# One of a step's fourth powers moves from ScalarE to VectorE, in the last of four attention loops

## The reference, cut to what matters

```
a = jnp.einsum('bhnd,bhmd->bhnm', q, k) ** degree      # degree 4
a = jnp.tril(a)
denom = jnp.sum(a, axis=-1, keepdims=True)
return jnp.einsum('bhnm,bhmd->bhnd', a / denom, v)
```

## Time and profile before

| what | value |
|---|---|
| median of 3 runs | 1062.55 us (1060.91 to 1063.41) |
| the profiled execution's own time | 1058.89 us |
| its span | 1057.1 us |
| busy in the span | PE 940.5 us (89%), DVE 716.9 (68%), ACT 570.6 (54%), POOL 529.0 (50%) |
| fourth powers, ScalarE (line 985) | 160 instructions, 74.8 us, 481 ns mean |
| fourth powers, VectorE (line 1568) | 96 instructions, 56.1 us, 609 ns mean |
| the fourth loop | from 428.3 to 517.7 us of the span |

### The profile page before, as it was taken

How to read it: one execution, slowest core, us unless ns; L and a number is a source line. 1 busy time by engine, 2 the same in 40 slices (tenths; PEclk the granted TensorE clock), 3 DMA queues, 4 the chain that set the end, 5 groups by cost and what they waited for, 6 DMA issues and landing times.

```text
span 1057.1 us, 21153 instructions
## 1 busy us (share of the span) xinstructions
PE 940.5 (89%) x5788; PEld 454.0 (43%) x5789; DVE 716.9 (68%) x1614; ACT 570.6 (54%) x1044; POOL 529.0 (50%) x749
## 2 busy tenths in 40 slices
PE   7989999899898999887788889999999999989992
PEld 5443334334343434342244445455455444444450
DVE  3887976787889778748848666555656565555561
ACT  2358884788847886777445234434344443333340
POOL 0006664564526665557402304665676665656642
PEclk9998999999999999967889899999999999999996
DMA  8213333434323443745458896998999898878884
GB/s 307 86 40 120 121 120 120 171 129 160 122 101 130 150 154 129 301 157 188 154 170 266 311 322 203 224 219 205 224 227 225 222 217 207 199 199 201 210 205 70
DMA packets 76301, 192.53 MB, mean 182 GB/s; under 512 B 10000, under 2 KB 11152, under 8 KB 74960
## 3 DMA queue, kind: packets, MB, share of 16 engines
q1 hardware_dynamic: 58544, 149.05, 42.0%
q0 software_dynamic: 17696, 42.72, 20.3%
HBM read 130.91 MB, written 60.83 MB: 181 GB/s over the span
## 4 chain that ended last, share of the span: by engine, by line
PE 31%; issue 14%; DVE 14%; DMA 13%; ACT 11%; POOL 8%; POOLq 5%; DVEq 3%; SPq 0%; ACTq 0%
DMA out<-yy,sidx 11%; PE bank L518 8%; PE bank L812 5%; PE bank L594 4%; PE bank L583 4%; ACT arena L993 3%; POOL wr L1202 3%; POOLq L1245 2%; PE bank L833 2%; POOLq L1201 2%; PE bank L533 1%; ACT s_p L985 1%; POOL s_p L1167 1%; DMA x1r<-x_scratch 1%; DVE s_p L1568 1%
## 5 line engine op out<-in xcount | busy, mean ns | idle before, releaser
L812 PE MATMUL bank<-arena,xgT 128*128 (+1 forms) x1140 | 283.4, 386 | 4.3 <-ACT xgT L1129 3.1
L1167 POOL TENSOR_TENSOR s_p<-s_p,c_causal 128x128 f32<-128x128 f32 x256 | 148.6, 604 | 218.3 <-DVE s_p L1568 187.2
L1122 ACT ACTIVATE hT<-bank 128x512 f16<-128x512 f16 x95 | 56.7, 597 | 280.6 <-PE bank L822 280.6
L518 PE MATMUL bank<-arena 128*128 128x512 f32 x384 | 184.6, 630 | 11.6 <-ACT arena L947 4.6
L812 PEld LDWEIGHTS bank<-arena,xgT 128*128 128x128 f16 x1140 | 107.4, 99 | 127.9 <-issue 39.7
L1175 POOL TENSOR_TENSOR arena<-arena 128x768 f16<-128x768 f32 x68 | 116.4, 1712 | 90.5 <-ACT arena L890 90.1
L1226 POOL DMA_INDIRECT out<-yy,sidx x79 | 126.7, 1604 | 36.5 <-issue 30.1
L833 PE MATMUL bank<-wd,hT 128*128 128x512 f16 x570 | 140.5, 383 | 0.7 <-ACT hT L1122 0.7
L993 ACT ACTIVATE arena<-bank 128x512 f32<-128x512 f32 (+3 forms) x256 | 101.2, 440 | 59.6 <-PE bank L568 59.6
L1881 DVE TENSOR_SCALAR yy<-bank,hsc 128x512 f32<-128x512 f32 x79 | 59.3, 751 | 107.7 <-DMA out<-yy,sidx 107.5
L518 PEld LDWEIGHTS bank<-arena 128*128 128x128 f32 x384 | 73.4, 199 | 103.2 <-issue 89.2
(11 more groups left out here) (196 smaller groups left out, 1389.1 us busy)
## 6 DMA issues: line engine op xcount, KB each, us to landing
wd<-w_scratch SPq DMA_DIRECT2D x81, 512.0 KB
arena<-w_experts SPq DMA_DIRECT2D x34, 768.0 KB, 5.9
w_scratch<-arena SPq DMA_DIRECT2D x34, 768.0 KB, 4.5
arena<-w_scratch SPq DMA_DIRECT2D x17, 1024.0 KB, 8.2
xin<-x SPq DMA_DIRECT2D x4, 1024.0 KB, 5.5
arena<-x SPq DMA_DIRECT2D x4, 1024.0 KB, 5.6
x_scratch<-arena SPq DMA_DIRECT2D x4, 1024.0 KB, 5.5
xg<-xn_scratch SPq DMA_DIRECT2D x16, 256.0 KB, 5.5
```

Of the source, the lines that this page charges most:

```text
L518: mm = pe.matmul(bk[:], xnT[:, c, m * P:m * P + P], wqkv[:, c, w * E:w * E + E], start=(c == 0), stop=(c == EC - 1))
L812: mm = pe.matmul(bank[2 + k][:], xgT[:, k, xh * EC + c, :], w, start=(c == 0 and xh + wh == 0), stop=(c == EC - 1 and xh == 1))
L1167: pool.tensor_tensor(d, d, C["causal"][:], ALU.mult).then_inc(p4_masked, 1)
```

## The change

In the fourth loop ScalarE takes the fourth power of head 3 only; that of head 1 goes to VectorE, which now makes heads 0, 1 and 2, one after another. It is one instruction in each of 16 steps. The semaphores follow: GpSimd's mask of head 1, and ScalarE's next square of head 1, now wait for VectorE's count.

```
-        act_fourths = lambda b, i: (0, 1, 2, 3) if 0 < b < B - 1 and i >= 8 else (1, 3)
+        act_fourths = lambda b, i: (0, 1, 2, 3) if 0 < b < B - 1 and i >= 8 else (1, 3) if b < B - 1 else (3,)
...
                     square(b, i, 2)
-                    fourth(b, i, 1)
+                    if 1 in act_fourths(b, i):
+                        fourth(b, i, 1)
                     square(b, i, 3)
```

## The result

| | before | changed |
|---|---|---|
| median | 1062.57 us (22 runs, 1058.71 to 1070.54) | 1066.15 us (22 runs, 1060.50 to 1073.53) |
| ratio | 1 | 1.0038, 95% interval 1.0021 to 1.0056 |
| the profiled execution's own time | 1058.89 us | 1070.85 us |
| its span | 1057.1 us | 1068.4 us |

The change costs about 4.0 us by the ratio (0.38% of 1062.57; the interval is 2.2 to 6.0); the medians lie 3.6 us apart. The forecast was 6.2 us, 1068.7. The ratios leave out executions in a slower state, which in all these runs are two of e4's twelve: 1534.83 us at a mean granted clock of 0.55, and 1074.67 us. The changed kernel's profile caught a long execution (own time 4.7 us above its median), so its span is no measure of the change.

What follows compares the result with a forecast made beforehand. No engine was full; hand-overs bound the loop, the path on ScalarE in steps 1 to 4, VectorE from step 8. Terms 0.6 + 1.0 - 0.2 + 3.5 + 1.3 = +6.2 us gave median 1068.7 us, range 1062.3 to 1071.0.

Steps and rivals of the forecast that it cites:

- VectorE is the path in steps 8 to 15: Fourth loop, steps 8 to 15: VectorE's added fourth powers lengthen the path by 2 x 1.76 = 3.5 us.
- rival A: Addition mostly swallowed: line 1175 keeps its place, 0.65 us in steps 8 to 15, 0 before; 1063.2 us, chance 0.17.
- Step 9 costs 1.3 us above its price: Step 9: line 1175 goes in before line 1358, so VectorE waits 1.64 us in place of 0.32; +1.3 us.
- The turns of steps 1 and 2: Steps 1 and 2: line 1175 goes in before the last of VectorE's four instructions; +1.0 us at step 4.
- +0.6 us for steps 0 to 4: Steps 0 to 4: VectorE's added work in steps 0 and 4, with ScalarE's -0.9 us in steps 1 to 3.
- The plain term: The +0.6 us for steps 0 to 4, from instruction prices and a mask's turn in step 4.
- Steps 5 to 7: Fourth loop, steps 5 to 7: TensorE is full and only hands the delay on; ScalarE gains 0.2 us in step 7.
- Rival C: Faster: ScalarE's lead reaches TensorE in step 4 before the clock falls; -4.1 us, 1058.5 us, chance 0.08.
- Nothing happens behind the loop: After the fourth loop: the expert layer begins with what the loop leaves, so the shift goes through to the end.
- The sum: Whole program: 0.6 + 1.0 - 0.2 + 3.5 + 1.3 = +6.2 us, median 1068.7 us.
- The signs named for single places: First masks of steps 8 and 12 still about 0.83 us; step 12 to 13 longer than 5.94 us by about 0.5.
- the forecast's own test: Prediction wrong if step 15's first mask comes less than 3 us later, or the program's end hides the loop's delay.

Runs made afterwards that it cites:

- e4: The changed kernel without step 9: head 1's fourth power on VectorE in all other steps of the fourth loop; ratio to before 0.9974 (0.9950 to 0.9998).
- e5: The kernel before, with GpSimd's line 1175 cut to 16 of 768 columns in the whole fourth loop; one run, 1051.92 us.
- e6: The changed kernel, with GpSimd's line 1175 cut to 16 of 768 columns in the whole fourth loop; one run, 1057.18 us.
- e3: The kernel before, with head 1's fourth power on VectorE in step 9 of the fourth loop only; ratio to before 0.9994 (0.9970 to 1.0019).
- e9: The changed kernel, with line 1175 cut to 16 of 768 columns in steps 1, 2 and 9 of the fourth loop only; one run, 1070.95 us.
- e7: The kernel before, with ScalarE making all four fourth powers in steps 8 to 15 of the fourth loop; median 1058.03 us, ratio 0.9948.

## Why the prediction was right in its time, point by point

- *VectorE is the path in steps 8 to 15, the moved instructions cost 3.5 us there.* Right in kind, a little high: the steps from 8 to 15 give +3.75 us in all (39.80 before, 43.55 changed), of which step 9 is 1.9, so the other six give 1.85 where their prices sum to 2.8. Step 11 cost 0.05 us for 0.24 forecast. With line 1175 cut (e5 to e6) the same six steps give +3.2, above their prices, so rival A had a true part: its waits took 0.9 us in by the prices, and 1.4 by e5 and e6. The changed kernel shows how, in step 7, where a small VectorE instruction (line 1380) takes 1.59 us beside line 1176 (0.18 before) and step 8's first fourth power is then free to start and takes 0.69 us (1.70 before).
- *Step 9 costs 1.3 us above its price, since line 1175 comes a turn early.* Right in mechanism, place and size: +1.9 us against 0.5 + 1.3 forecast (e3, e4, e9).
- *The turns of steps 1 and 2, +1.0 us (0 to 1.6), and +0.6 us for steps 0 to 4.* The turns are right in mechanism: the last of line 1328 and of 1573 waits for 1176, and e9 removes both waits. The sum arrived as +1.3 us, not 1.6, with the two terms wrong in opposite ways: e9, where the turns are gone, finishes the group 0.14 us earlier than the kernel before (forecast +0.6), so the turns were worth 1.46. The plain term took ScalarE's 0.9 us off a path that moved to VectorE, and called the chain of 435.0 to 450.9 us ScalarE's squares, where it also holds its fourth powers, high halves and norm rows.
- *Steps 5 to 7: TensorE is full and only hands the delay on.* This step failed. TensorE's time there depended on its clock, the low stretch shrank from 20.5 to 6.8 us, and 4.6 us were given back. Rival C had the right size (1.5 us a block of logits, measured 1.33 and 1.63) and the wrong cause: it wanted an earlier arrival, the clock went with a later one.
- *Nothing happens behind the loop.* Not quite. The projection's first matmul is 1.4 us late and the expert layer's first 1.4 to 2.6 us; the clock is at its low level for 3.4 us at the start of the last projection in both executions of the changed kernel and in the second of the one before, and not in the first, which is most of the spread.
- *The sum.* The loop as a whole gave +0.8 us at step 15, not +6.2; the program gave +4.0 (2.2 to 6.0). Between the expert layer's first matmul (+1.4 to +2.6) and the end another 1.4 to 2.6 us stay unexplained; the length of the expert layer ranged from 506.6 to 518.6 us over the profiles, 509.5 and 513.5 us for the kernel before alone, so single profiles can't tell. The signs named for single places came true: the first masks of steps 8 and 12 take 0.84 us, and from step 12's first fourth power to step 13's it is 6.38 us (5.94 before). By the forecast's own test (step 15's first mask at least 3 us later) its account of the loop is wrong as a whole. The time fell in its range and on its side; that it came near the median is luck, owed to two misses of opposite sign: the clock gave 4.6 us back in steps 5 to 7, and some 3.2 us came on top behind step 15 (4.0 less 0.8), of which 1.4 to 2.6 are the unexplained ones.

## What to carry to other kernels

Before moving work to VectorE, list what GpSimd runs beside it: where both alternate on SBUF operands, an added instruction can cost its own length and also the turn it takes. A long GpSimd instruction that so comes one turn early costs the difference to the short one it displaces (here 1.64 us for 0.32). Elsewhere a wait that is there already can take the added work in. Look for the places where a long one has only just come last (here by 0.2 us), price each, and test them with one kernel that changes that step alone. Relieve the engine that the chain of waits names in the stretch at hand (e7), not the one with the larger busy share, and take the granted clock of every stretch in the chain as something that the change can move.

## What the runs showed of the hardware that I had not expected

One fourth power of half a microsecond costs 1.9 us (e3). Cutting one GpSimd line of 1.64 us, 16 times, to 16 columns makes a loop of 87 us 12 us shorter (e5), of which some 4.5 us came with a higher clock. No row of idle time shows the waits on that line: they are inside the instructions' own durations (VectorE's line 1359 takes 1.97 us beside it and 0.79 without; the fourth loop's masks took 3.6 us more at the same count). A delay of 1.3 us before TensorE's work resumed went with a low-clock stretch of 6.8 in place of 20.5 us, five profiles against seven, with one exception (e5); the four pieces of TensorE's work in it took 5.97 in place of 10.54 us.
